# The passage from the attention groups to the expert tiles in a ViT tower: another order, silu in one step earlier, list tables with step one

## What is computed

```python
h = _L0_tok_ref(x, W, b, cls_token, pos_embed)                  # 64 x 37 x 256
h = _layernorm(h + _L0_attn_ref(h, Wq, Wkv, Wout, b_out, pos_emb))
# _L0_ffn_ref, on N = 64 * 37 = 2368 tokens xf:
scores = jax.nn.softmax(xf @ router_w, axis=-1)
topk_scores, topk_idx = jax.lax.top_k(scores, TOP_K)            # TOP_K = 2 of 8
combine = jnp.zeros((N, E)).at[jnp.arange(N)[:, None], topk_idx].add(topk_scores)
g = jnp.einsum('nh,ehf->enf', xf, gate_w)
u = jnp.einsum('nh,ehf->enf', xf, up_w)
y = jnp.einsum('enf,efh->enh', jax.nn.silu(g) * u, down_w)
routed = jnp.einsum('enh,ne->nh', y, combine)
shared = jax.nn.silu(xf @ shared_gate_w) * (xf @ shared_up_w) @ shared_down_w
h = _layernorm(h + shared + routed)
```

## Time and profile before

| | us |
|---|---|
| median of 3 runs | 737.69 |
| profiled execution, its own time | 737.93 |
| its span | 736.2 |
| busy: TensorE | 717.0 |
| busy: TensorE's weight loads | 621.1 |
| busy: VectorE | 527.8 |
| busy: ScalarE | 385.4 |
| busy: GpSimd | 120.1 |
| mean granted clock of TensorE | 0.994 |

### The profile page before, as it was taken

The page is one execution under the profiler, slowest core; times in us unless marked ns, Lnnn a source line. Parts: engine busy times, 40 slices in busy tenths (PEclk is TensorE's granted clock), DMA queues, the critical chain, the costliest instruction groups (busy, mean ns, idle before and its releaser), DMA issues. The chain is left out here.

```text
span 736.2 us, 14656 instructions
## 1 busy us (share of the span) xinstructions
PE 717.0 (97%) x5106; PEld 621.1 (84%) x5107; DVE 527.8 (72%) x1111; ACT 385.4 (52%) x745; POOL 120.1 (16%) x156
## 2 busy tenths in 40 slices
PE   8999999999999999999999999999989999999996
PEld 5887897979889797979979796777879999999885
DVE  3377998989898898989889899977952222222667
ACT  1556657464756746474674655522216555553363
POOL 2000000000000000000000000000024777774130
PEclk9999999999999999999999999999999999999998
DMA  8961001010101001010100005210011222221811
GB/s 271 310 192 36 2 26 49 26 48 25 48 1 39 34 25 48 25 36 0 36 1 25 13 26 173 68 38 10 0 32 57 81 82 87 82 76 34 277 68 52
DMA packets 27532, 47.11 MB, mean 64 GB/s; under 512 B 3626, under 2 KB 18768, under 8 KB 27500
## 3 DMA queue, kind: packets, MB, share of 16 engines
q1 hardware_dynamic: 22928, 36.65, 15.8%
q0 software_dynamic: 4224, 9.71, 4.1%
q10 hardware_dynamic: 348, 0.34, 0.1%
HBM read 35.40 MB, written 13.12 MB: 66 GB/s over the span
## 5 line engine op out<-in xcount | busy, mean ns | idle before, releaser
L715 POOL TENSOR_TENSOR rs<-ve,neg_half 111x2 f32<-111x2 f32 x11 | 12.2, 1109 | 455.3 <-DVE ve L1828 455.3
L1276 PE MATMUL ps_S<-attnT,v_sb 128*128 128x128 f32 x704 | 85.9, 275 | 0.1
L1736 DVE COPY_PREDICATED table<-bit,table 111x112 f32<-111x112 int16 (+6 forms) x110 | 75.1, 683 | 11.2
L2163 DVE COPY attnT<-ps_S 128x256 f32<-128x256 f32 x44 | 18.7, 425 | 89.7 <-PE ps_S L1290 89.6
L1276 PEld LDWEIGHTS ps_S<-attnT,v_sb 128*128 128x128 f32 x704 | 82.2, 192 | 0.3 <-issue 0.3
L888 PE MATMUL ps_X<-wkv_sb,hT 128*111 128x512 f32 (+1 forms) x176 | 80.4, 598 | 0.0
L932 PE MATMUL ps_X<-oT,wout_sb 128*128 128x222 f32 x320 | 61.9, 351 | 0.0
L932 PEld LDWEIGHTS ps_X<-oT,wout_sb 128*128 128x128 f32 x320 | 60.1, 190 | 0.2 <-issue 0.2
L813 PE MATMUL ps_S<-hT,wq_sb 128*128 128x216 f32 (+1 forms) x320 | 58.5, 340 | 0.0
L888 PEld LDWEIGHTS ps_X<-wkv_sb,hT 128*111 128x111 f32 (+1 forms) x176 | 28.5, 173 | 35.5 <-issue 34.2
L732 POOL DMA_INDIRECT attn<-h_d,ids_x x44 | 45.2, 1027 | 69.3 <-issue 61.3
(11 more groups left out here) (312 smaller groups left out, 1367.5 us busy)
## 6 DMA issues: line engine op xcount, KB each, us to landing
down_sb<-in_x_dram SPq DMA_DIRECT2D x10, 648.0 KB
gu_sb<-y_d SPq DMA_DIRECT2D x8, 512.0 KB, 6.9
h_d<-hT SPq DMA_DIRECT2D x11, 222.0 KB, 2.5
kept<-h_d SPq DMA_DIRECT2D x11, 222.0 KB, 2.5
h_d<-h SPq DMA_DIRECT2D x10, 222.0 KB
wkv_sb<-in_L_attn_Wkv_dram SPq DMA_DIRECT2D x2, 1024.0 KB, 12.0
gu_sb<-in_L_ffn_gate_w_dram SPq DMA_DIRECT2D x2, 1024.0 KB, 11.2
gu_sb<-in_L_ffn_up_w_dram SPq DMA_DIRECT2D x2, 1024.0 KB, 11.7
```

The lines of the kernel that those rows point to most:

```text
L1276: mm = nc.tensor.matmul(S[:, i, j * FF + f * P:j * FF + f * P + P], held[:, i, k, j, f * P:f * P + P], xgT[:, i, k], start=(k == 0), stop= ...
L1736: A.did(V.copy_predicated(near[:, :, :, 0:SL - d], by_side(bit[:, n], r)[:, :, :, 0:SL - d], near[:, :, :, d:SL]))
```

## The change

- **Last pair.** TensorE issues `turn(1)` ahead of the two halves of `residual(9)` and `turn(2)` between them, then `turn(3)` and `turn(4)`, and `route(0)` and `route(1)` after a wait for the readers of the residual (`res_ready`), then `turn(5)` and `turn(6)`. ScalarE evicts turns 1 and 2 ahead of `softmax_exp(20)`.
- **After it.** VectorE runs `shared(0, 2)`, the norm of the last pair and `shared(1, 0)` before `slots(0)`, and the following steps in another order. TensorE routes chunks 7 to 9 and transposes their logits ahead of `shared_out(0)`.
- **Silu.** `late(c, f)` holds from part 1 of chunk 2 on.
- **List tables.** `tile_hot` is now (choice, 2 x 44 tiles, 20 half chunks) and no longer (choice, 20, 88). The tile numbers (`tile_wide`, spread by a GpSimd copy), the tile of each token and the parts of the numbers are bf16, with the half chunk as the innermost dimension. The list matmuls read `tile_hot[:, j, :, t]`, 88 elements 20 elements apart.

```diff
@@ -201,7 +201,8 @@
         id_hi = sb("id_hi", [P, TOPK, NROW])
-        id_lo = sb("id_lo", [P, TOPK, NROW])
+        id_parts = sb("id_parts", [P, 2, TOPK, NROW], BF16)
+        tile_of = sb("tile_of", [P, TOPK, NROW], BF16)
         ids_f = sb("ids_f", [P, TOPK, NROW])
@@ -229,7 +230,8 @@
                      whole_numbers(bit, "p i h a -> p (i h a)", TOPK, NROW - EARLY, P)]
-        tile_hot = whole_numbers(oT, "p f r -> p (f r)", TOPK, NROW, 2 * NT)
+        tile_hot = whole_numbers(oT, "p f r -> p (f r)", TOPK, 2 * NT, NROW)
+        tile_wide = whole_numbers(ex, "p h a -> p (h a)", 1, NT, NROW)[:, 0]
         second = sb("second", [P, NT])
@@ -334,6 +336,7 @@
         tiles_hot = sem("tiles_hot")
+        tile_numbers = sem("tile_numbers")
         sh_gu = sem("sh_gu")
@@ -477,7 +480,10 @@
         BEFORE = FULL - 2
-        LATE = 3
+        def late(c, f):
+
+            return (c, f) > (2, 0)
+
         N_TABLES = 7
@@ -748,6 +754,8 @@
             norm(G2 - 1)
+            nc.gpsimd.tensor_copy(tile_wide, tile_no[:, :NT].unsqueeze(2).to_broadcast([P, NT, NROW])
+                                  ).then_inc(tile_numbers, 1)
             pool.wait_ge(h1_stored, 16 * (G2 + 1))
@@ -1088,11 +1096,21 @@
                 pe.wait_ge(v_ready, p * 4 + 3)
-                residual(p - 1, X[:, 1])
                 if ahead:
+                    residual(p - 1, X[:, 1])
                     keys(p + 1)
                 else:
-                    for c in range(1, FULL):
+                    turn(1)
+                    pe.wait_ge(ot_sb, p * 4)
+                    residual_half(p - 1, X[:, 1], 0)
+                    turn(2)
+                    residual_half(p - 1, X[:, 1], 1).then_inc(res_done, 1)
+                    for c in range(3, 5):
+                        turn(c)
+                    pe.wait_ge(res_ready, p * KE)
+                    for c in range(2):
+                        route(c)
+                    for c in range(5, FULL):
                         turn(c)
@@ -1108,9 +1126,6 @@
                 if not ahead:
-                    pe.wait_ge(at_sb, 4 * (G - 1))
-                    for c in range(2):
-                        route(c)
                     pe.wait_ge(ot_sb, 2 * G - 2)
@@ -1214,7 +1229,7 @@
                     for j in range(TOPK):
-                        mm = nc.tensor.matmul(E[:, 1, :2 * NT], place_hot[b][:parts, j, at], tile_hot[:parts, j, t],
+                        mm = nc.tensor.matmul(E[:, 1, :2 * NT], place_hot[b][:parts, j, at], tile_hot[:parts, j, :, t],
                                               start=(t == 0 and j == 0), stop=(t == NROW - 1 and j == TOPK - 1))
@@ -1233,16 +1248,18 @@
             turn(FULL + 1)
-            shared_hidden(1, 2, 4)
+            shared_hidden(1, 2, 3)
             turn(NEW)
-            shared_out(0)
-            for c in range(FULL, NCH):
+            for c in range(FULL, NCH - 1):
                 route(c)
-            shared_hidden(2, 0, 1)
+            route(NEW)
+            shared_hidden(1, 3, 4)
             pe.wait_ge(across_sb, 7)
             by_half(EARLY, NROW)
-            shared_hidden(2, 1, 4)
+            shared_out(0)
+            shared_hidden(2, 0, 2)
             rank(1, EARLY, NROW)
+            shared_hidden(2, 2, 4)
             shared_out(1)
@@ -1506,12 +1523,15 @@
                 gates(p, 1)
+                if not ahead:
+                    for c in range(1, 3):
+                        turn(c)
                 softmax_exp(p * 2)
                 else:
-                    for c in range(1, FULL):
+                    for c in range(3, FULL):
                         turn(c)
@@ -1544,7 +1564,7 @@
                     act.wait_ge(sh_hid, at - 1)
-                if c >= LATE:
+                if late(c, f):
                     nc.scalar.activation(thS[:, f % 2, :width(c)], bank[:, :width(c)], ACT.Silu).then_inc(sh_tanh, 1)
@@ -1565,14 +1585,13 @@
             turn(FULL + 1)
-            for f in range(2, FC):
-                shared_tanh(1, f)
+            shared_tanh(1, 2)
             turn(NEW)
                 logits_out(c)
-            shared_tanh(2, 0)
+            shared_tanh(1, 3)
             router_exp(1, EARLY, NROW)
-            for f in range(1, FC):
+            for f in range(FC):
                 shared_tanh(2, f)
@@ -2002,7 +2021,8 @@
                 R.settle(0)
-                R.did(V.scalar_tensor_tensor(id_lo[:], id_hi[:], -64.0, id_left[:], ALU.mult, ALU.add))
+                R.did(V.scalar_tensor_tensor(id_parts[:, 1], id_hi[:], -64.0, id_left[:], ALU.mult, ALU.add))
+                R.did(V.tensor_copy(id_parts[:, 0], id_hi[:]))
                 R.settle(0)
@@ -2015,19 +2035,19 @@
                 R.settle(0)
-                R.did(V.tensor_tensor(of_tile[:], of_tile[:], slotf[:], ALU.add))
+                R.did(V.tensor_tensor(tile_of[:], of_tile[:], slotf[:], ALU.add))
                 R.settle(0)
 
-                by_tile = [P, NROW, NT]
-                is_tile, hi = tile_hot[:, j, :, NT:], tile_hot[:, j, :, :NT]
-                R.did(V.tensor_tensor(is_tile, tile_no[:, :NT].unsqueeze(1).to_broadcast(by_tile),
-                                      of_tile[:, j].unsqueeze(2).to_broadcast(by_tile), ALU.is_equal))
+                by_tile = [P, NT, NROW]
+                is_tile, hi = tile_hot[:, j, NT:], tile_hot[:, j, :NT]
+                R.did(V.tensor_tensor(is_tile, tile_wide, tile_of[:, j].unsqueeze(1).to_broadcast(by_tile),
+                                      ALU.is_equal))
                 R.settle(0)
-                R.did(V.tensor_tensor(hi, is_tile, id_hi[:, j].unsqueeze(2).to_broadcast(by_tile), ALU.mult))
+                R.did(V.tensor_tensor(hi, is_tile, id_parts[:, 0, j].unsqueeze(1).to_broadcast(by_tile), ALU.mult))
                 R.settle(0)
-                V.tensor_tensor(is_tile, is_tile, id_lo[:, j].unsqueeze(2).to_broadcast(by_tile), ALU.mult
+                V.tensor_tensor(is_tile, is_tile, id_parts[:, 1, j].unsqueeze(1).to_broadcast(by_tile), ALU.mult
                                 ).then_inc(tiles_hot, 1)
@@ -2111,24 +2131,24 @@
             residual(G2 - 1, S[:, 2])
-            slots(0, 0, EARLY)
             shared(0, 2)
             shared(1, 0)
+            slots(0, 0, EARLY)
+            shared(1, 1)
             places_of(0, 0, 0, EARLY)
-            shared(1, 1)
+            shared(1, 2)
+            choose(1, EARLY, NROW)
+            shared(1, 3)
+            shared(2, 0)
+            shared_sum(0)
+            slots(1, EARLY, NROW)
+            shared(2, 1)
             ids_apart()
-            shared(1, 2)
+            shared(2, 2)
             places_of(0, 1, 0, EARLY)
-            shared(1, 3)
-            shared_sum(0)
-            shared(2, 0)
-            choose(1, EARLY, NROW)
-            for f in range(1, 3):
-                shared(2, f)
-            slots(1, EARLY, NROW)
             shared(2, 3)
@@ -2140,6 +2160,8 @@
                         tile_of_each()
+                    if c == 3 and f == 2:
+                        dve.wait_ge(tile_numbers, 1)
                     if c == 3 and f >= 2:
```

## The result

The changed kernel takes 739.19 us (median of 20 runs), the kernel before 737.77 (20 runs): a ratio of 1.0021 (95% interval 1.0015 to 1.0026), slower by 1.42 us. Forecast were 733.9 and a range of 732.2 to 736.3. The profiled span is 737.4 us, with TensorE busy for 721.4.

What follows compares the result with a forecast made beforehand. TensorE, busy 97% of the span, was taken as the bound. Terms -0.33 - 0.59 - 0.17 - 2.31 - 1.85 + 1.5 = -3.75 us gave 733.9 us against a median of 737.69, range 732.2 to 736.3.

Steps and rivals of the forecast that it cites:

- what the tables' layout costs TensorE: List matmuls reading elements 40 bytes apart: a doubling of TensorE's column time, 40 x 37 ns, costing 1.5 us.
- my upper bound: List matmuls streaming at VectorE's whole strided rate of 1.8 ns per element: 158 ns each, costing 4.8 us.
- my own sign of being wrong: Prediction called wrong if list matmuls stand 39 or over 150 ns apart, route(2) does not wait, or the lists wait again.
- the clock: Behind the lists: with no 2 us of idle time in front, the clock stays at 2.4 GHz, gaining 1.85 us.
- dear: Rival at the 40 list matmuls: 737.2 us at 158 ns, 738.8 at 200 ns; 5% slower, 4% no change.
- Turns: Last pair's turns and first routes: 1.75 us of idle time moves to route(2), and 0.33 us is gained.
- shared(0,2) before slots, norm, second choice: Waits of 0.59 us before turn(FULL) and 0.17 us before the second rank go; no other TensorE wait comes.
- Silu: One VectorE operation for two, three times: 1.35 us off VectorE; the 1.28 us table load covered by ScalarE's waiting.
- Tables on VectorE: Six list-table operations at 0.72 us instead of 1.07, done at 534.6, so TensorE's 2.31 us wait at the lists goes.
- no faster: Rival on VectorE's list tables: operations stay at 1.07 us, TensorE waits 1.15, no clock dip; 735.0 us, 10%.
- The gather as a floor: Behind the lists: were they 1.5 us shorter, TensorE would wait 0.1 to 0.2 us for the first gathered tile.

Runs made afterwards that it cites:

- e1: Changed kernel with the list tables of before (float32, 88 elements side by side); order, turns and silu as changed: 734.42 us, ratio 0.9958.
- e2: Kernel before with the new list tables alone: 740.67 us, ratio 1.0043.
- e3: Changed kernel with two half chunks innermost in the tables, (10, 88, 2), so TensorE reads elements 4 bytes apart: 733.21 us, ratio 0.9939.
- e6: Changed kernel with five half chunks innermost in the tables, elements 10 bytes apart: 734.66 us, one run.
- e4: Changed kernel with four half chunks innermost in the tables, elements 8 bytes apart: 734.10 us, ratio 0.9951.
- e9: Changed kernel (elements 40 bytes apart) with eight hidden matmuls of chunk NEW spread among the list matmuls: 738.80 us, ratio 1.0017.
- e7: Kernel of e3 with the old order of turns and first two routes in the last pair: 733.06 us, ratio 0.9940.
- e10: Kernel before with the list tables of e3, old order, old turns, silu from chunk 3: 734.46 us, ratio 0.9957.
- e11: Kernel of e3 with silu in one step from chunk 3 only: 733.16 us, one run.
- e8: Kernel of e3 with ScalarE evicting outputs(20) ahead of distance(21) in the last pair: 731.78 us, ratio 0.9922.

## Why the prediction was wrong

**The step that failed** is "what the tables' layout costs TensorE". I took a doubling, 1.5 us. The matmuls went to four times, 158 ns: 6.51 us, where with the same order and the elements side by side they take 1.77 (e1), so 4.74. e1 and e2 show that it is the tables, e3 to e6 that it is the step and how it goes with it. I had the number: 158 ns was my upper bound, at the rate at which VectorE read with a step of 56 bytes, and over 150 ns was my own sign of being wrong. I chose the lower value by comparing TensorE's own column time with VectorE's element. That was an argument with no row. The only rows said what an element costs VectorE at such a step (1.8 ns), not what factor it makes. That TensorE came out at the same 1.8 ns no run explains; that the bound was met exactly may be luck. The Trainium skill, page SBUF — State Buffer, section on the DMA port swizzle, puts the distance that is free at 8 bf16. For TensorE's moving operand the measurements differ, and they decide: elements 4 bf16 apart (8 bytes, e4) doubled the matmul, elements 2 apart (e3) cost nothing.

**The step that hung on it** was the clock. I booked 1.85 us for it because the idle time would go. It went, and the clock fell all the same, for longer: 4.10 - 2.11 = 1.99 on the hidden matmuls and 0.37 on the output layer, 2.36 paid. e9 shows the cause: full-rate matmuls among the slow ones keep it at 1.00. The 1.85 itself was too high: I took 39 ns for the last twelve list matmuls at the full clock, and e1 has 57. Against e1 the fall in the kernel before cost 2.21 - 1.77 = 0.44 on the lists and 3.22 - 2.11 = 1.11 on the hidden matmuls, 1.55 us. It may also not be in every run of that kernel: of 33 runs of it, the twelve with a mean granted clock of 0.997 or more took 737.0 us on average, the other 21 took 737.8. The clock at the kernel's end moves that mean too, so this is a hint only. In the rival "dear" I priced 158 ns at 737.2, no change, and set the turning point at 131 ns more; with the clock counted, 119 ns more already gave 739.2. That rival was the right one, held at 5 + 4%, and priced short by the clock.

**What held.**
- *Turns.* The idle time moved to route(2) as forecast: 1.8 us, released by ScalarE's oT. The gain was 0.13 (e7) for my 0.33: I had set my start of turn_weights(20), 472.13, built from starts in the timeline, against 472.46 in the chain of waits, where the timeline has 472.29, so that only 0.16 was left.
- *shared(0,2) before slots, norm, second choice.* The waits of 0.59 and 0.17 went, and no new one came. In all TensorE reached the lists 1.57 us earlier (e10 against e3) for my 1.09. The modelled tails of matmuls hide some 0.17 of a wait each time; the rest I didn't trace.
- *Silu.* VectorE reaches the tables 1.25 us earlier (e11: 531.30 after 453.32, e3: 529.78 after 453.05) and nothing follows. The table load stands beside waits of ScalarE: in the changed kernel it starts at 514.08, one activation behind a wait of 4.65 us and one ahead of a wait of 1.8.
- *Tables on VectorE.* 0.61 to 0.62 us, my value 0.72. The estimate by the Trainium skill, page VectorE: DVE Perf Modes, section on the perf-mode tier table, was 0.61, and the trace agrees. Tables were done 1.4 us before TensorE came. My terms for VectorE's path add up to 16.3 us and not to 16.5, and the wait in the rival "no faster" to 1.04 and not 1.15; neither changes the forecast.
- *The gather as a floor.* 0.2 us of waiting in e3.

**The sum.** Forecast -3.75, in the traces +1.48, a difference of 5.23. It is 3.24 for the operand (4.74 for 1.5) and 2.66 for the clock (2.36 paid in place of 1.55, so +0.81 for -1.85), less 0.67 by which the part before the lists gained more (4.07 for 3.40).

## What to carry to other kernels

A layout that makes one engine fast is read by another: price both, and first in the engine on the path. Between VectorE's need (16-bit, step one, if only in runs of two) and TensorE's (four elements to a 16-byte line) there was a layout that serves both, (10, 88, 2) for (88, 20): 6 us better than the changed kernel. And an idle time that goes may only have moved: look up what the next instruction behind it waits for, as at route(2), where the cure was the order on another engine (e8).

## What the runs showed of the hardware

- A strided bf16 moving operand costs TensorE as if it were read in 16-byte lines: 88 columns take 39 to 40 ns x max(1, 4 / elements in a line), the same at 20 and 40 bytes (e1 to e6; one trace for each step). 158 / 88 = 1.8 ns, a little over four columns at 2.4 GHz.
- The slow matmuls hardly mind the clock: the last twelve took 175 ns each with it at 0.50 in the changed kernel ((541.43 - 539.33) / 12) and 173 with it at 1.00 in e9 ((543.72 - 541.64) / 12). What suffers are the full-rate ones behind them: sixteen hidden matmuls took 4.10 us for 2.11.
- TensorE can count as busy for 100% of a stretch and lose its clock in it (536 to 546 in the changed kernel). No fall followed 1.36 us of idle time in e1, 1.67 in e9 and 1.8 at route(2) in the changed kernel; one followed the 2.3 before the lists in the kernel before, and none where e10 removes that wait in the same order.
- A tensor_tensor on VectorE whose second input repeats a run of two elements (e3) is as fast as with runs of twenty, 0.61 us for 880 elements. With runs of five (e6) it took 0.70.
